# Running sums over edge columns on one Trainium2 core: each column's VectorE operation becomes two, on halves of the features, with a semaphore for each half

## What is computed

```python
# layer 0: attention with 8 heads        layer 2: attention with 4 heads
alpha = softmax over the edges of one dst of leaky_relu(a_src[src] + a_dst[dst])
out   = segment_sum(x[src] * alpha, dst)
# layer 1: three times (features 128, 256, 128)
agg   = segment_sum(x[src], dst)
# layer 3: three times (features 128)
out   = segment_sum(xw[src] * norm[:, None], dst)
```

## Time and profile before

| What | Value |
|---|---|
| median of three timed runs | 10415.89 us (10411.06 to 10423.69) |
| the profiled execution | 10436.18 us, span 10433.9 us |
| POOL busy | 6862.1 us, 66% |
| DVE busy | 3439.7 us, 33% |
| ACT busy | 1484.0 us, 14% |
| PE busy | 421.8 us, 4% |
| DMA engines, mean over the span | 99 GB/s |

### The profile page before, as it was taken

How to read it: one execution, slowest core, us unless ns; L and a number is a source line. 1 busy time by engine, 2 the same in 40 slices (tenths; PEclk the granted TensorE clock), 3 DMA queues, 4 the chain that set the end, 5 groups by cost and what they waited for, 6 DMA issues and landing times. The chain is left out here.

```text
span 10433.9 us, 25725 instructions
## 1 busy us (share of the span) xinstructions
PE 421.8 (4%) x2048; PEld 303.3 (3%) x2048; DVE 3439.7 (33%) x8044; ACT 1484.0 (14%) x3624; POOL 6862.1 (66%) x6765
## 2 busy tenths in 40 slices
PE   2000000000300004000010000000001000000000
PEld 1000000000200002000010000000000000000000
DVE  4444452222233331222234444622222222222223
ACT  1000001001121111100000000022221222212221
POOL 4666637777477763777656666177775777667774
PEclk7555555555655557555555555555555555555555
DMA  3333313222355541322213333032222322222222
GB/s 97 106 104 108 101 58 98 94 94 92 106 194 188 187 171 57 96 93 93 87 51 100 95 99 102 26 96 98 94 93 79 96 93 93 88 86 94 93 93 72
DMA packets 359329, 1035.33 MB, mean 99 GB/s; under 512 B 118369, under 2 KB 200010, under 8 KB 323178
## 3 DMA queue, kind: packets, MB, share of 16 engines
q0 software_dynamic: 242832, 506.98, 18.4%
q1 hardware_dynamic: 116314, 526.71, 12.8%
HBM read 518.01 MB, written 515.19 MB: 99 GB/s over the span
## 5 line engine op out<-in xcount | busy, mean ns | idle before, releaser
L262 POOL DMA_INDIRECT gb<-rows,src x6256 | 6375.9, 1019 | 3005.6 <-issue 1968.1
L355 DVE SCALAR_TENSOR_TENSOR gb<-gb,mask,psum 128x128 f32<-128x128 f32 (+1 forms) x4686 | 1733.1, 370 | 4668.5 <-remote 1903.8
L337 ACT ACTIVATE psum<-gb,weight 128x128 f32<-128x128 f32 x2346 | 837.1, 368 | 2463.7 <-issue 1724.3
L1079 DVE SCALAR_TENSOR_TENSOR gb<-gb,mask,psum 128x136 f32<-128x136 f32 (+1 forms) x1492 | 527.6, 354 | 621.0 <-DVE gb L1079 339.5
L339 ACT COPY psum<-gb 128x512 f32<-128x512 f32 (+2 forms) x823 | 423.0, 561 | 1858.0 <-DMA gb<-rows,src 1554.2
L279 POOL DMA_INDIRECT gb<-runs,end_row x392 | 375.6, 958 | 154.0 <-issue 117.1
L1074 DVE TENSOR_TENSOR psum<-gb,psum 128x408 f32<-128x408 f32 (+4 forms) x546 | 306.8, 562 | 242.3 <-DVE gb L1079 149.8
L1008 ACT ACTIVATE psum<-running 128x192 f32<-128x192 f32 (+3 forms) x72 | 20.7, 288 | 2346.0 <-DVE running L1064 2173.8
L364 PE MATMUL psum<-gb,carry_from 128*128 128x128 f32 (+2 forms) x12 | 5.2, 534 | 6795.1 <-DVE gb L355 6795.1
L646 POOL DMA_INDIRECT spread<-acc,spread_row x98 | 94.4, 963 | 228.7 <-DVE spread_row L917 118.1
L364 PEld LDWEIGHTS psum<-gb,carry_from 128*128 128x128 f32 x12 | 3.0, 310 | 6796.6 <-DVE gb L355 5509.9
(11 more groups left out here) (221 smaller groups left out, 1622.1 us busy)
## 6 DMA issues: line engine op xcount, KB each, us to landing
runs<-gb SPq DMA_DIRECT2D x132, 1472.0 KB
gb<-rows,src POOLq DMA_INDIRECT x6256
runs<-gb SPq DMA_DIRECT2D x45, 2176.0 KB
runs<-gb SPq DMA_DIRECT2D x33, 1748.0 KB
runs<-gb SPq DMA_DIRECT2D x33, 1610.0 KB
runs<-gb SPq DMA_DIRECT2D x33, 1483.5 KB
rows<-acc SPq DMA_DIRECT2D x48, 256.0 KB
gb<-runs,end_row POOLq DMA_INDIRECT x392, 2.5
```

Of the source, the lines that this page charges most:

```text
L262: m.s_rows[b % BUFS].up(nc.gpsimd.indirect_dma_start(m.batch(b, columns, row)[:, j, 0:width], None, table, bass.IndirectOffsetOnAxis(ap=m. ...
L337: last = nc.scalar.activation(out[:, j - j0, :], rows[:, j, 0:width], ACT.Copy, scale=m.weight[:, r:r + 1])
L355: m.s_column.up(nc.vector.scalar_tensor_tensor(rows[:, j, 0:width], before, m.mask[:, r:r + 1], fed[:, j - j0, :], ALU.mult, ALU.add))
L1079: m.s_column.up(nc.vector.scalar_tensor_tensor(rows[:, j, 0:S], before, m.mask[:, r + j:r + j + 1], fed[:, j - j0, :], ALU.mult, ALU.add))
```

## The change

A second semaphore, `s_column2`, counts columns like `s_column`. The operation of a column becomes two on the first and the second half of its features (64 + 64, 128 + 128 in the wide pass, 68 + 68 and 66 + 66 in the attention passes). The first half waits for and raises `s_column`, the second `s_column2`, so that the half of one column waits only for the same half of the column before. Every other place that waited for `s_column` now waits for both.

```diff
@@ pass_gathers
             pool.wait_ge(m.s_column.sem, m.s_column.at(batches[b - BUFS + 1][0] + 1))
+            pool.wait_ge(m.s_column2.sem, m.s_column2.at(batches[b - BUFS + 1][0] + 1))
@@ store_runs, and likewise in the sync block of attention_layer
         sp.wait_ge(m.s_column.sem, m.s_column.at(first + size))
+        sp.wait_ge(m.s_column2.sem, m.s_column2.at(first + size))
@@ feed_sums
             act.wait_ge(m.s_column.sem, m.s_column.at(start + end))
+            act.wait_ge(m.s_column2.sem, m.s_column2.at(start + end))
@@ running_sums
-            if r == 0:
-                m.s_column.up(nc.vector.tensor_scalar(rows[:, 0, 0:width], fed[:, 0, :], 1.0, None, ALU.mult))
-            else:
-                before = rows[:, j - 1, 0:width] if j else row_before(m, b, columns, row)[:, 0:width]
-                m.s_column.up(nc.vector.scalar_tensor_tensor(rows[:, j, 0:width], before, m.mask[:, r:r + 1], fed[:, j - j0, :],
-                                                             ALU.mult, ALU.add))
-            dve.wait_ge(m.s_column.sem, m.s_column.count)
+            for half, count in enumerate((m.s_column, m.s_column2)):
+                part = slice(half * (width // 2), (half + 1) * (width // 2))
+                if r == 0:
+                    count.up(nc.vector.tensor_scalar(rows[:, 0, part], fed[:, 0, part], 1.0, None, ALU.mult))
+                else:
+                    before = rows[:, j - 1, part] if j else row_before(m, b, columns, row)[:, part]
+                    dve.wait_ge(count.sem, count.count)
+                    count.up(nc.vector.scalar_tensor_tensor(rows[:, j, part], before, m.mask[:, r:r + 1], fed[:, j - j0, part],
+                                                            ALU.mult, ALU.add))
@@ carry_sums
     pe.wait_ge(m.s_column.sem, m.s_column.at(COLS))
+    pe.wait_ge(m.s_column2.sem, m.s_column2.at(COLS))
@@ attention_layer, the columns on DVE
-                        before = rows[:, j - 1, 0:S] if j else m.carried[:, 0:S]
-                        m.s_column.up(nc.vector.scalar_tensor_tensor(rows[:, j, 0:S], before, m.mask[:, r + j:r + j + 1],
-                                                                     fed[:, j - j0, :], ALU.mult, ALU.add))
-                        dve.wait_ge(m.s_column.sem, m.s_column.count)
+                        for half, count in enumerate((m.s_column, m.s_column2)):
+                            part = slice(half * (S // 2), (half + 1) * (S // 2))
+                            before = rows[:, j - 1, part] if j else m.carried[:, part]
+                            dve.wait_ge(count.sem, count.count)
+                            count.up(nc.vector.scalar_tensor_tensor(rows[:, j, part], before, m.mask[:, r + j:r + j + 1],
+                                                                    fed[:, j - j0, part], ALU.mult, ALU.add))
```

More of the change, by code:

```diff
@@ L162, in __init__ @@
         self.s_column = signal("s_column")
+        self.s_column2 = signal("s_column2")
         self.s_fed = signal("s_fed")
@@ L1077, in _ @@
                     for j in range(j0, j0 + n):
-                        before = rows[:, j - 1, 0:S] if j else m.carried[:, 0:S]
-                        m.s_column.up(nc.vector.scalar_tensor_tensor(rows[:, j, 0:S], before, m.mask[:, r + j:r + j + 1],
-                                                                     fed[:, j - j0, :], ALU.mult, ALU.add))
-                        dve.wait_ge(m.s_column.sem, m.s_column.count)
+                        for half, count in enumerate((m.s_column, m.s_column2)):
[4 more added lines that the diff above has]
+                                                                    fed[:, j - j0, part], ALU.mult, ALU.add))
+            dve.wait_ge(m.s_column.sem, m.s_column.count)
+            dve.wait_ge(m.s_column2.sem, m.s_column2.count)
             m.s_dve_turn.up(nc.vector.tensor_copy(end_top, heads_of(m.top, K)[:, :, size]))
```

## The result

The change makes the kernel slower: 10944.51 us (median of four runs, 10939.38 to 10946.33) beside 10417.92 us for the kernel before, a ratio of 1.0506 with a 95% interval of 1.0489 to 1.0523. Forecast were 10748 us and a range of 10400 to 11300.

The account below looks back on a forecast made before the run. Bound: operations delivered to an engine once per 1.40 us after POOL gathers some 35 us without rest. Terms 2 x 47 + 3 x 41 + 45 + 27 + 43 = 332 us on 10416 gave 10748 us; range 10400 to 11300.

Parts of the forecast that it names:

- a semaphore's way back: First rival: the semaphore's return lasts 1.40 us, so both halves travel at once, attention rests go; 10100 us, chance 0.13.
- no change: Third rival: earlier cure or longer cycles leave 1.39 to 1.40 us a column in sum passes; about 10420 us, chance 0.09.
- a shared line of deliveries: Fourth rival: POOL and DVE share deliveries 0.70 us apart, so a column takes 2.10 us; 14900 us, chance 0.06.
- the likeliest case: The forecast itself: DVE falls behind at slow delivery and POOL rests; 10748 us, own range 10520 to 10980, chance 0.50.
- Narrow sum passes: Passes 1, 3, 5, 6, 7: 92 columns take 131 us with a 16 us rest; 1128 us, +47 or +41 each.
- at 123 quick delivery returns: Narrow-pass step: POOL stops at 115 us, 8 us of rest restore quick delivery, and POOL restarts at 131.
- Columns delivered quickly: DVE's two halves overlap when delivery is quick, so a column costs 0.31 us, against 0.38 before.
- the pair of operations 0.20 us apart: Sign for overlapping halves: two independent operations start 0.20 us apart though the first lasts 0.29.
- Halves that don't overlap: Second rival: a quickly delivered column takes 0.62 us, attention passes 1264 us; 10990 us in all, chance 0.18.
- Attention passes: Passes 0 and 4: a 17 us rest in every three batches; 1170 us a pass, +27 and +43.
- Wide pass: 34 operations against 21.25 us of gathers, the narrow passes' ratio, so the same 1.424 us a column: +45 us.
- Other edits: Second waits of POOL, SP, ACT and PE pass at once, hidden behind rests, under 10 us if not; counted as nothing.

Follow-up runs that it names:

- e1: Kernel before plus a one-element memset, with its own semaphore, behind each column's whole operation: 10823.8 us, ratio 1.0396.
- e3: Kernel before plus one more, long-passed semaphore wait for DVE ahead of each column's operation: 10426.2 us, one run.
- e2: The change with its two chains made one, each half waiting for the half ahead of it: 11110.3 us, ratio 1.0660 to the kernel before.
- e13: The change in attention passes; kernel before plus a signal-free memset into unused PSUM per column in sum passes: 9298.8 us beside 9298.7 for the kernel before.
- e4: Kernel before plus three one-element memsets behind each column's operation: 9300.5 us, one run, beside 9282.07 for the kernel before.
- e8: Kernel before plus a one-element memset behind each column's operation that raises and waits for no semaphore: 9281.9 us beside 9282.07, ratio 1.0015.
- e5: Kernel before with a batch's sums made in two DVE scans, ACT copying into and out of PSUM: 10628.4 us, ratio 1.0207.
- e11: Second version with scans against the kernel before; ACT repeats the mask, weighted rows go to PSUM first, two PSUM slots: 10290.5 us, ratio 0.9869.
- e6: Kernel before with each column's operation at half width in the six sum passes, second half's sums left out: 9279.6 us, one run, beside 9282.07.

## Why the prediction was right, and where its sizes were off

**The mechanism** was right on chips like that of the result. DVE's operations come one per 1.40 us once POOL has gathered for some time; 46 of them don't fit beside 23 gathers; POOL gathers at 1.25 us and rests every fourth batch. e1 makes the same rests without halves, e3 shows that waits play no part, and the rivals of a semaphore's way back, of no change and of a shared line of deliveries (10100, 10420 and 14900 us) are far off. 10944 lies at the upper end of the likeliest case's own range, 10520 to 10980; the sum passes (1152 to 1155 us) and attention passes (1201 and 1211) end just above the 1110 to 1150 and 1150 to 1200 that were to show it.

**Narrow sum passes: 1128 forecast, 1152 measured.** The step that failed is "at 123 quick delivery returns", 8 us into the rest. It returned after 14.5 us, the rest was 20 us and not 16, and four batches took 135 us and not 131: 1.467 us a column. That 8 us were needed was read from a single rest of an attention pass. A second term hid a third of this: eight such rounds took 1082 us, 34 more than forecast, but the last 46 gathers took 70 us where 80.5 were forecast (46 x 1.424 + 15). The other end was right: quick delivery ended 34.2 us after the restart, where 35 were assumed.

**Columns delivered quickly: 0.31 us forecast, 0.386 measured,** as long as a whole column before (0.38). I took the pair of operations 0.20 us apart as a sign that halves overlap, and not as the least distance between any two. Halves start 0.193 us apart at best; so two fill the time of the one they replace, and halving gains nothing even where nothing is delivered slowly. The sum hardly felt it. On the rule of the Trainium skill, "VectorE: DVE Perf Modes", section "The DRAIN you can't avoid", the trace sides with its exception: independent halves overlap, 0.193 us apart with 0.28 us of duration, while the dependent ones of e2 stand 0.323 apart.

**Halves that don't overlap** (the second rival, 10990) were tried as e2: 11110. Its attention passes were about right (1264 us forecast for each, 1261 and 1238 measured). In the sum passes it had the same 8 us before the cure, some 1137 us for a narrow pass where 1160 came, and is too small by the same step.

**Attention passes: 1170 forecast, 1211 and 1201 measured.** I had a rest of 17 us every three batches. It is 13 to 14 us every two: two restarts 70.15 us apart with 46 gathers between them, 1.525 us a column (timeline of POOL in pass 0).

```profile
684.13 0.94 POOL L264 DMA_INDIRECT gb<-rows,src  x1 [13.56 <-DMA runs<-gb]
...
754.28 0.94 POOL L264 DMA_INDIRECT gb<-rows,src  x1 [12.88 <-DVE gb L1090]
```

The step was that quick delivery lasts until 30 us or more after the restart (8 quick operations of batch m); here operations began to come 1.4 us apart 15 to 22 us after it. The cure took 5 to 8 us, as assumed.

So neither length is a constant. The cure took longest where POOL had gathered longest: 5 to 8 us after 46 gathers here, up to 10.7 after 69 in e2, 13.6 to 14.7 after 92 in most rests of the narrow passes. That is close to 0.15 us for each gather (6.9, 10.4 and 13.8 us), and 0.15 is what a gather of 1.25 us is quicker than the mean of 1.40: as if the rest had to make up for what the gathers were ahead. This is an estimate fitted to these rests, no run tests it, and in the wide pass it is too long (12.8 us after 85 gathers, 8 to 11 seen). But both figures stood in the earlier trace rows, and would have given 14 us for four batches where I took 8.

**Wide pass: +45 forecast, +72 measured.** The step was to take over 1.424 us a column from the narrow passes: up to the short last batches it was 1.470, there as here. The rests are not the same, though: they come after four or five batches and at times after one more, 6 to 18 us long.

**Other edits and the stretches between passes: 0 forecast, -46 us measured.** The stretches run from the last gather of a pass to the first of the next, and make up 40 of the 46; the rest lies behind the last pass. Probably DVE is less far behind at a pass's end, with a rest just past; no run tests that, and I had not looked at these stretches.

**"What causes it I don't know"** was the weakest place, and it decides more than any term: in three of six groups of runs the same kernel never gets slow, takes 9.28 to 9.30 ms, and the change, by its attention passes (e13) and by e4 and e8 in the sum passes, would cost next to nothing. The change as a whole didn't run on such a chip. What makes the chips differ the runs don't tell, and it need not be the chip alone: on the quicker chips one of e13's ten executions took 10298.5 us where the other nine took 9296 to 9301, and two of e8's ten took 9397 and 9498 (none of the three was profiled). Open too: whether an operation has to raise a semaphore or write SBUF to be delivered slowly, and whether its width matters.

## What to carry to other kernels

Halving an operation to hide its latency pays only down to the least distance between two operations, which was 0.19 us here; look for that before counting on overlap. If operations reach an engine slowly while GpSimd issues indirect DMAs, the number of operations beside each gather decides, not their length: here a memset of 0.06 us for each column cost nearly as much as the halving, and more waits cost nothing. And the first thing to find out is whether the slow delivery belongs to the kernel or to the chip it was traced on: run the kernel before on several.

## What I had not expected of the hardware

- The same kernel takes 10402 to 10438 us on some chips and 9280 to 9308 on others, 12% apart, and its executions in each group agree within 0.3%. On the first kind POOL's gathers fall from 1.25 to 1.40 us on average after 184 of them without a rest, and DVE's and ACT's operations to one per 1.40 us; on the second nothing of this happens.
- On the first kind 598 gathers took 1.40 us each although DVE got one operation in 3.4 us, and though most single gathers were near 1.25 us apart. It is a bound on the mean: where the change's rests or e5's held gathers bring the mean over 1.40 anyway, the others are back at 1.25.
- A DVE TENSOR_TENSOR that reads two wide operands from SBUF (5.12 us) held a gather until it was done, 5.78 us; beside one with an operand in PSUM (1.70 us) gathers took 0.94 to 1.24 us (e11).
- Three more DVE operations for each column disappear in the 0.38 us of the column where nothing is delivered slowly: a narrow pass takes 975 to 978 us with none (e6, whose column operations have half the width), one (e8) and three memsets (e4).
